# Perceiver layer on one core: context tiles turned by VectorE and a transfer through DRAM instead of by TensorE

## The reference, cut to what matters

```python
x = x + xattn(layernorm(x), ctx_1024, ...)     # 16 heads of 64, 16 batches
# inside xattn
ctx = layer_norm(context) * g + b              # [16, 1024, 256]
k, v = split(ctx @ Wkv)                        # 2 x 1024 columns
k = apply_rope(k, cos, sin)                    # [x1*cos - x2*sin, x2*cos + x1*sin]
attn = softmax(clip(q @ k.T / 8, -11, 11))     # per batch and head 64 x 1024
out = (attn @ v) @ Wo + bo
```

## Time and profile before

| | us |
|---|---|
| median of 3 runs (1255.79 to 1260.7) | 1257.02 |
| the profiled execution | 1255.76 |
| its span | 1254.0 |
| PE busy | 1226.5 (98% of the span) |
| DVE busy | 936.9 (75%) |
| ACT busy | 704.7 (56%) |
| POOL busy | 678.9 (54%) |
| granted TensorE clock, mean | 0.998 of full speed |

### The profile page before, as it was taken

How to read it: one execution, slowest core, us unless ns; L and a number is a source line. 1 busy time by engine, 2 the same in 40 slices (tenths; PEclk the granted TensorE clock), 3 DMA queues, 4 the chain that set the end, 5 groups by cost and what they waited for, 6 DMA issues and landing times.

```text
span 1254.0 us, 40596 instructions
## 1 busy us (share of the span) xinstructions
PE 1226.5 (98%) x16508; PEld 1027.6 (82%) x16508; DVE 936.9 (75%) x1924; ACT 704.7 (56%) x1359; POOL 678.9 (54%) x611
## 2 busy tenths in 40 slices
PE   7999999999999999999999999999999999999997
PEld 3678888888888888888888888888888788789997
DVE  6797877777887777877777787777777356768886
ACT  7756556555655655655655665665643233356664
POOL 3466666666576566566566566666554123333333
PEclk9999999999999999999999999999999999999999
DMA  6345444545445445445444444444545261566662
GB/s 235 66 99 114 99 107 110 107 100 114 101 98 114 104 108 115 103 98 113 105 106 105 108 101 105 111 106 102 132 99 130 88 219 36 187 178 194 205 186 73
DMA packets 96913, 149.95 MB, mean 120 GB/s; under 512 B 29452, under 2 KB 64728, under 8 KB 96600
## 3 DMA queue, kind: packets, MB, share of 16 engines
q1 hardware_dynamic: 92648, 143.14, 46.2%
q0 software_dynamic: 4080, 4.22, 1.7%
HBM read 66.20 MB, written 14.83 MB: 65 GB/s over the span
## 4 chain that ended last, share of the span: by engine, by line
PE 92%; ACT 2%; DVE 2%; DMA 2%; issue 1%; POOL 1%; SPq 0%; POOLq 0%; ACTq 0%; DVEq 0%
PE bank L1421 30%; PE bank L1451 28%; PE bank L1407 11%; PE bank L1759 6%; PE bank L1476 3%; PE bank L1431 2%; PE bank L1587 2%; PE bank L1809 2%; PE bank L1811 1%; PE bank L1810 1%; PE bank L1616 1%; PE bank L1659 1%; PE bank L1510 1%; DMA w_two<-in_L_ffn_W_dram 1%; PE bank L1640 1%
## 5 line engine op out<-in xcount | busy, mean ns | idle before, releaser
L568 POOL TENSOR_TENSOR kr<-kr,ksw 128x1024 f32<-128x1024 f32 x128 | 308.7, 2412 | 341.7 <-DVE pr L969 219.3
L1421 PE MATMUL bank<-ct,wk_hi 128*128 128x512 f32 x1024 | 331.7, 405 | 0.0
L1451 PE MATMUL bank<-p_hi,xc 128*128 128x512 f32 x1024 | 315.8, 390 | 0.0
L720 ACT ACTIVATE ctf<-bank,vecs 128x128 f32<-128x128 f32 x256 | 103.3, 453 | 333.5 <-PE bank L1431 333.5
L1451 PEld LDWEIGHTS bank<-p_hi,xc 128*128 128x128 f32 x1024 | 191.9, 188 | 39.9
L1421 PEld LDWEIGHTS bank<-ct,wk_hi 128*128 128x128 f32 x1024 | 182.3, 188 | 41.8
L1421 PE MATMUL bank<-ct,wk_lo 128*128 128x512 f32 x512 | 200.6, 392 | 0.0
L1451 PE MATMUL bank<-p_lo,xc 128*128 128x512 f32 x512 | 200.5, 392 | 0.0
L1001 DVE TENSOR_TENSOR kw<-bank,stab 128x512 f32<-128x512 f32 x256 | 175.7, 686 | 27.7 <-PE bank L1421 24.8
L992 DVE TENSOR_TENSOR p_lo<-pr,p_hi 128x1024 fp32r<-128x1024 f32 x128 | 184.3, 1440 | 1.8 <-ACT p_hi L707 1.8
L1009 DVE TENSOR_TENSOR ct<-ctf,ct 128x256 fp32r<-128x256 f32 x128 | 57.8, 452 | 170.6 <-ACT ct L725 170.6
(11 more groups left out here) (215 smaller groups left out, 1728.8 us busy)
## 6 DMA issues: line engine op xcount, KB each, us to landing
ksw<-kw SPq DMA_DIRECT2D x512, 128.0 KB
raw<-in_ctx_dram SPq DMA_DIRECT2D x64, 256.0 KB, 4.0
w_two<-in_L_ffn_W_dram SPq DMA_DIRECT2D x15, 1024.0 KB, 5.1
x_slots<-fill SPq DMA_DIRECT2D x128, 64.5 KB, 2.9
w_all<-in_L_ffn_W_dram SPq DMA_DIRECT2D x4, 2048.0 KB, 17.6
wo<-in_L_ffn_W_dram SPq DMA_DIRECT2D x7, 1024.0 KB, 5.2
lsum<-l_rows SPq DMA_DIRECT2D x64, 64.0 KB, 2.7
xs<-x_slots SPq DMA_DIRECT2D x23, 129.0 KB, 2.2
```

The costliest lines, as they stand in the source:

```text
L568: pool.tensor_tensor(kr[:, i], kr[:, i], ksw[:, i], ALU.add).then_inc(kr_done, 1)
L720: last = act.activation(ctf[:, k], psT[:, k * P:(k + 1) * P], ACT.Identity, bias=vecs[:, 3, k:k + 1], scale=vecs[:, 2, k:k + 1])
L1421: last = pe.matmul(psK[:, a * 512:(a + 1) * 512], l[:, k, w], ct[:, h % 3, r, k], start=(m == 0), stop=(m == len(parts) - 1))
L1451: last = pe.matmul(psZ[c], xc[:, slot_, l, t, cols], r[:, i, :, t], start=(f == 0 and m == 0), stop=(f == 1 and m == len(parts) - 1), skip ...
```

## The change

Tiles 0 to 7 (batch 1) are turned by TensorE as before. Tiles 8 to 127 take another way. VectorE turns the eight 32x32 blocks across and four down of the normalised tile, each within itself, into `xt` (`blocks_turned`, tile `j + 11`, between `weights_low` and `divided`). After every fourth tile, in steps with j % 4 = 1, SP writes `xt` to DRAM with four DMAs of 32 partitions in runs of 128 floats; these stand ahead of the key exchange of the step. Behind the exchange SP waits until they have landed and loads the half, now with the 256 values on the partitions, into `ctf` (2 x 512 floats per partition). In the next step (j % 4 = 2) ScalarE scales `ctf` in place and rounds it into `ct` high, and VectorE makes `ct` low of all 1024 floats at once. The columns of a half now stand in another order, which the cosine and sine multiplications undo by reading the keys in PSUM in runs of 32. Moments, shift and normalising run two steps earlier, context loads start two steps earlier, the loads of `wout_raw` and `bout_all` and the clearing of `vbd` move to the last steps.

```diff
+        x_turned = nc.dram_tensor("x_turned", [KC, P, HALF_S], F32, kind="Internal").ap()
+            xt = sb("xt", [P, D // HALF, HT, HALF], F32, turning)
+            ctf = sb("ctf", [P, KC, HALF_S], F32, turning)
...
@@ SP, step(j)
+                if due(j, 1) and (j + 7) // 4 < 2 * B:
+                    h = (j + 7) // 4
+                    sp.wait_ge(xt_done, HT * (h - 1))
+                    wait(sp, xt_moved, 80 * (h - 2))
+                    for i in range(4):
+                        sp.dma_start(x_turned[:, :, i * P:(i + 1) * P].rearrange("c (k p) s -> p (c k) s", p=HALF),
+                                     xt[i * HALF:(i + 1) * HALF].rearrange("p k t s -> p k (t s)")).then_inc(xt_moved, 16)
                 if there(j + 2):
                     ...
                         sp.dma_start(ksw[to:to + HALF, i], kw[of:of + HALF, i]).then_inc(sw_ld[i], 16)
+                if due(j, 1) and (j + 7) // 4 < 2 * B:
+                    h = (j + 7) // 4
+                    sp.wait_ge(xt_moved, 80 * (h - 2) + 64)
+                    wait(sp, ct_lo_done, HT * h)
+                    sp.dma_start(ctf[:], x_turned.rearrange("c p s -> p c s")).then_inc(xt_moved, 16)
...
@@ ScalarE, step(j)
-                if there(j + 9):
+                if 0 <= j + 9 < ST:
...
+                if due(j, 2) and (j + 6) // 4 < 2 * B:
+                    h = (j + 6) // 4
+                    act.wait_ge(xt_moved, 80 * (h - 1))
+                    for k in range(KC):
+                        last = act.activation(ctf[:, k], ctf[:, k], ACT.Identity, bias=vecs[:, 3, k:k + 1], scale=vecs[:, 2, k:k + 1])
+                    last.then_inc(ctf_done, 1)
+                    if h >= 3:
+                        act.wait_ge(k_ps, 2 * last_key(h - 3) + 2)
+                    act.wait_ge(ctf_done, ST + h - 1)
+                    act.copy(ct[:, h % 3, 0], ctf[:]).then_inc(ct_hi_done, HT)
...
@@ VectorE
+            def blocks_turned(j):
+                if ST <= j + 11 and there(j + 11):
+                    n = j + 11
+                    dve.wait_ge(xhat_done, n + 1)
+                    if n % HT == 0:
+                        wait(dve, xt_moved, 80 * (n // HT - 3) + 64)
+                    dve.transpose(xt[:, :, n % HT], raw[:, n // ST % 2, n % ST].rearrange("p (k s) -> p k s", s=HALF)).then_inc(xt_done, 1)
...
-                    dve.tensor_tensor(kw[:, i, cols], psK[:, cols], stab[:, places], ALU.mult).then_inc(kw_done, 1)
-                    dve.tensor_tensor(kr[:, i, cols], psK[:, cols], ctab[:, places], ALU.mult).then_inc(ku_done, 1)
+                    keys_ = psK[:, cols].rearrange("p (i t s) -> p t i s", t=HT, s=HALF)
+                    dve.tensor_tensor(by_tile(kw[:, i, cols]), keys_, by_tile(stab[:, places]), ALU.mult).then_inc(kw_done, 1)
+                    dve.tensor_tensor(by_tile(kr[:, i, cols]), keys_, by_tile(ctab[:, places]), ALU.mult).then_inc(ku_done, 1)
...
+                if due(j, 2) and (j + 6) // 4 < 2 * B:
+                    h = (j + 6) // 4
+                    dve.wait_ge(ct_hi_done, HT * (h + 1))
+                    dve.tensor_tensor(ct[:, h % 3, 1], ctf[:], ct[:, h % 3, 0].bitcast(F32), ALU.subtract).then_inc(ct_lo_done, HT)
...
@@ TensorE
             def turn_context(j):
-                if there(j):
+                if 0 <= j < ST:
...
-                    if due(j - 9, 7):
-                        pe.wait_ge(o_sum, (j - 16) // 4 * 2 + 1)
```

More of the change, by code:

```diff
@@ L83, in build @@
         fill = sb("fill", [P, D + 2])
+        with ExitStack() as turning:
+            xt = sb("xt", [P, D // HALF, HT, HALF], F32, turning)
+            ctf = sb("ctf", [P, KC, HALF_S], F32, turning)
         wout_raw = sb("wout_raw", [P, KC, D])
         bo_all = sb("bo_all", [P, D])
-        with ExitStack() as turning:
-            ctf = sb("ctf", [P, KC, P], F32, turning)
         bout_all = sb("bout_all", [P, D])
+        with ExitStack() as middle:
+            vbd = sb("vbd", [P, 2, AH, 2 * (AD + 1)], F32, middle)
+        h_lo_0 = sb("h_lo_0", [P, 2 * AH * 2 * (AD + 1)], F32R)
         vec_rows2 = sb("vec_rows2", [E * FT + 4, P])
@@ L91, in build @@
         feat_w = sb("feat_w", [P, 2, P])
-        with ExitStack() as middle:
-            vbd = sb("vbd", [P, 2, AH, 2 * (AD + 1)], F32, middle)
-        h_lo_0 = sb("h_lo_0", [P, 2 * AH * 2 * (AD + 1)], F32R)
         square = sb("square", [P, P])
@@ L390, in _ @@
             sp.dma_start(x_slots[E * TOK:, :], fill[:]).then_inc(fill_st, 16)
-            for r in range(KC):
-                for h in range(2):
-                    sp.dma_start(wout_raw[:, r, h * P:(h + 1) * P].rearrange("p (g d) -> p g d", d=AD),
-                                 Wout[r * P:(r + 1) * P, :].rearrange("p (g h d) -> p h g d", h=2, d=AD)[:, h]).then_inc(wout_ld, 16)
             sp.dma_start(vec_rows2[0:E * FT, :], b1.rearrange("e (f p) -> (e f) p", p=P)).then_inc(vec2_ld, 16)
@@ L422, in step @@
                     sp.dma_start(x_slots[j * N:(j + 1) * N, :], fill[o:o + N, :]).then_inc(fill_st, 16)
-                if j >= 0 and j % 2 == 0 and j // PAIRS + 2 < B:
-                    sp.wait_ge(xT_ps, j + 2)
-                    sp.wait_ge(x_lo_done, j + 2)
-                    context(j // PAIRS + 2, j % PAIRS // 2)
+                if j >= -2 and j % 2 == 0 and (j + 2) // PAIRS + 2 < B:
+                    if j + 2 < ST:
+                        sp.wait_ge(xT_ps, j + 4)
+                    else:
+                        sp.wait_ge(xt_done, j + 4 - ST)
+                    sp.wait_ge(x_lo_done, j + 4)
+                    context((j + 2) // PAIRS + 2, (j + 2) % PAIRS // 2)
             for j in range(-2, 0):
@@ L538, in _ @@
             pool.memset(cvec[:, 1:2], EPS)
-            pool.memset(vbd[:], 0.0).then_inc(vbd_ones, 1)
-            pool.wait_ge(vbd_ones, 1)
-            for b in range(2):
-                at = b * (AD + 1) + AD
-                pool.memset(vbd[b * N:(b + 1) * N, :, :, at:at + 1], 1.0).then_inc(vbd_ones, 1)
-                pool.wait_ge(vbd_ones, b + 2)
             for c in range(2):
@@ L681, in step @@
                     act.activation(pr_by_head, heads_by_tile, ACT.Exp, scale=SCALE).then_inc(exp_done, 1)
-                if there(j + 10) and j + 10 >= ST:
-                    i = (j + 10) % 2
-                    x_ = raw[:, (j + 10) // ST % 2, (j + 10) % ST]
-                    act.wait_ge(shift_done, j + 11 - ST)
-                    if j + 10 == ST:
+                if there(j + 12) and j + 12 >= ST:
+                    i = (j + 12) % 2
+                    x_ = raw[:, (j + 12) // ST % 2, (j + 12) % ST]
+                    act.wait_ge(shift_done, j + 13 - ST)
+                    if j + 12 == ST:
                         act.wait_ge(xhat_done, ST)
@@ L937, in normalised @@
             def normalised(j):
-                if 0 <= j + 10 < ST:
-                    n = j + 10
-                    dve.wait_ge(rstd_done, n + 1)
+                for n in range(max(j + 11, 0) if j > -10 else 0, min(j + 12, ST)):
+                    dve.wait_ge(rstd_done, (n // HT + 1) * ST)
                     dve.tensor_scalar(raw[:, 0, n], raw[:, 0, n], xl_mom[:, n, 0:1], xl_rsd[:, n:n + 1], ALU.subtract, ALU.mult).then_inc(xhat_done, 1)
             def shifts(j):
-                if ST <= j + 10 and there(j + 10):
-                    i = (j + 10) % 2
-                    dve.wait_ge(rstd_done, j + 11)
-                    if j + 10 >= ST + 2:
-                        dve.wait_ge(xhat_done, j + 9)
+                if ST <= j + 12 and there(j + 12):
+                    i = (j + 12) % 2
+                    dve.wait_ge(rstd_done, 2 * (j + 13))
+                    if j + 12 >= ST + 2:
+                        dve.wait_ge(xhat_done, j + 11)
                     dve.scalar_tensor_tensor(out=shift[:, i:i + 1], in0=mv[:, i, 0:1], scalar=-1.0, in1=rstd[:, i:i + 1],
@@ L952, in counted @@
             def counted(j):
-                if ST <= j + 11 and there(j + 11):
-                    n = j + 11
+                if ST <= j + 13 and there(j + 13):
+                    n = j + 13
                     b, t = n // ST, n % ST
@@ L1020, in step @@
                 weights_low(j)
+                blocks_turned(j)
                 divided(j)
```

88 lines of the change are left out of this document (50 added, 38 removed).

## The result

| | us |
|---|---|
| before, median of 16 runs (1255.34 to 1261.48) | 1257.95 |
| changed, median of 16 runs (1253.54 to 1274.22) | 1264.88 |
| ratio, with its 95% interval | 1.0045 [1.0024, 1.0065] |
| changed, the profiled execution | 1253.54, span 1251.8 |
| forecast (range) | 1243.0 (1228 to 1274) |

The changed kernel is 0.45% slower (0.2 to 0.7%), a difference too small to count, where 14 us (1.1%) of gain were forecast. One of the 16 runs (1274.22) is a slow one and is left out of the ratio. The profiled execution is the fastest of the 16, 11.3 us under their median, so I also read a second profile, taken with the first experiment (1262.71 us, span 1261.0).

A forecast was written before the change was run, and what follows sets the result against it. The prediction took PE, busy 98% of the span, as the bound. Turn removal -27.6 us plus new stall 13.5 gave -14.1: from 1255.76 to 1241.7, with the median 1.3 above, 1243.0 us; range 1228 to 1274.

The forecast's parts named there:

- PE's turn: Last in each PE step; removing it was to save 0.23 us for 120 of 128 tiles, 27.6 us.
- Block turn: On VectorE, after p_lo: taken as 0.42 us a tile, hidden up to about 0.9 us.
- Issue of a write: Block writes on SP ahead of the exchange: 0.59 us each; with 0.78, stall 30 us in all.
- The 200 us a quad to which I gave 1 in 100: Block writes to DRAM as slow as a strided transposing DMA: kernel about 6000 us longer, chance 1 in 100.
- The writes' landing: Four block writes, j % 4 = 1: landed 2.9 or 3.9 us after the last issue, before the next block turn.
- VectorE's wait: Before the next half's first block turn, for landed writes: nothing of its own, or about 0.2 us a quad.
- the ends: Earlier moments, moved small loads and vbd clearing beside other work: 0 us, bounds -1 to +2.
- stalls in other steps: PE idle at steps other than before the scores of j % 4 = 3: none forecast.
- the stall before T3: PE waiting for kr before the scores of j % 4 = 3: 0.45 us a quad, 13.5 us over 30 quads.
- The landing of the exchange: Key exchange, j % 4 = 1: landed at most 4.86 us after issue, in late cases for instance 5.82.
- The rival "given back": Slow write issue or exchange packets held up 0.7 us cancel the gain: 1251 to 1263 us, chance 0.18.
- The rival "slower": SP's queue in j % 4 = 1 makes the exchange the bound: 1275 us, +18 us, chance 0.22.

The follow-up runs named there:

- the first experiment: The changed kernel as it is, measured again for a second trace: median 1260.14 us, ratio 1.0028.
- No turn at all: The kernel before with TensorE's turn left out for tiles 8 to 127 and nothing in its place: 1232.17 us, ratio 0.9798.
- the best version: Changed kernel, two block writes on SP before clearing and context load, two on ScalarE, small loads divided between steps 118 and 119: 1235.46 us, ratio 0.9828.

## Why the prediction was wrong

Right first. **PE's turn**: 0.23 us in plain steps held exactly (6.98 to 6.76). In the step with outputs it is 0.40 (8.09 to 7.69), which the earlier trace rows could not show as a turn's price: a quad gains 1.09 us instead of 0.92. **Block turn**: 0.435 us against 0.42. **Issue of a write**: 0.46 us in the median (2.0 for four) against 0.61, so the unknown that I called the one that counts was no problem. The 200 us a quad to which I gave 1 in 100 did not come either. **The writes' landing**: the turn at T1 + 9.1, the upper of my two values (8.0 to 9.0); but VectorE's wait is 1.9 us on the mean and up to 3.7, not under 1.5. **Idle place**: before T3's scores, released by POOL, as listed.

What failed, and by how much in the spans of the two profiles: the ends 7.1 and 9.1 us, stalls in other steps 4.8 and 6.6, the stall before T3 2.5 and 8.0; the turn gave 2.3 more than forecast. Together that is the 11.9 and 21.1 us by which the forecast of -14.1 missed, within 0.3. By steps:

*The landing of the exchange, kept at its value before the change.* This is the term of the sum that was mis-sized. The prediction took 4.86 us for 73% of the quads and 5.82 for the rest, on the mean 5.1. The 4.86 of the earlier trace rows is only a bound, the smallest of the 21 quads in which VectorE released GpSimd, and it hit by luck: the landings read from the semaphore have a mean of 4.83 us in the kernel before, 5.0 to the start of the sum. In the changed kernel they have 5.37 and 5.40 (4.2 to 7.2). The forecast let the exchange land as before although four new transfers are in flight with it; that they would hold it up stood only in the rivals. Put into my own sum with its two starts, 5.77 and 6.7, the landings of the kernel before give 10.9 us of stall in 28 quads, those of the changed one 21.5 and 22.8. Measured: 16.0 and 21.5. So the 13.5 of the forecast came close in the first profile because it took the exchange's starts later than they were.

*Stalls in other steps, put at nothing.* 4.8 and 6.6 us. I took VectorE's delay as ending with its quad. It doesn't: when `kr` is late on GpSimd, it overlaps `p_lo` (2.55 us at 606.18 instead of 1.33), the block turn and the context's low part come later, and with them the next `kw` and its exchange, which starts at T2 + 5.9 in the median instead of T2 + 4.87. In the second profile 3.0 of the 6.6 us are two steps at a granted clock of 0.81.

*VectorE's wait "costs nothing of its own".* Nearly so: by the table above the clipping adds 1.4 and 2.6 us to what the exchange makes. But it would make 8.6 and 11.6 alone, so with the exchange early again it is the next to stall, and the remedy had to make both early.

*Ends, 0 with bounds -1 to +2.* Too low: 2.0 to 2.2 us up to step 7; 2.0 to 2.5 in steps 120 to 126, most of it the small loads ahead of an exchange, which I had put "beside other work" without looking at the queue; 2.9 to 4.6 behind them, about what the low clock can cost there. No turn at all has 2.0 of the last too, so not all of it is the change's.

*The clock.* No term at all. It is no further loss beside these but a part of them: up to 3.3 and 5.4 us of the ends, and 3.0 of the stalls in the second profile. The prediction also took 1.3 us from the profiled execution to the median; the first profile lay 11.3 under it.

The sum from parts measured: -29.9 (turn) + 20.8 (stalls) + 2.2 + 2.0 + 2.9 = -2.0 us in the first profile, against -2.2 in its span; -29.9 + 28.1 + 2.0 + 2.5 + 4.6 = +7.3 in the second, against +7.0. The rival "given back" came nearest (1264.88 and 1260.14, for 1251 to 1263). The slow issue that it named was no cause. An exchange held up by 0.7 us was one, with 0.5 to 0.6 us, by whichever transfer. The rival "slower" had the right place and overrated the price.

Open: why the first scores come 1.5 us later (53.04 against 51.53), why the stretch behind the cross attention has more of the low clock in every version, and which transfer holds the exchange up. No run was made for any of them.

## What to carry to other kernels

When a change uses up spare time, don't take the duration of the transfer it now waits for from one case. Where another engine was the releaser, the case gives only an upper bound, and where the transfer was, only the late ones are seen: 5.35 to 6.51 us to the start of the sum, median 5.80, in 9 of 30 quads here, against 5.0 on the mean of all. Then ask what the change adds beside that transfer, and price a longer landing in the forecast itself. When two inputs of one operation are both late, undoing one shows little, and moving a transfer's start does not show that its landing moved: read both inputs' times. Before a queue gets new work ahead of an urgent transfer, look at what stands before both and isn't urgent: moving two issues was worth about 20 us here (1260.14 to 1240.57, ratios 1.0028 and 0.9868).

## What the runs showed of the hardware

VectorE's `p_lo`, whose two inputs lie in SBUF, stretched from 1.33 to 2.55 us while GpSimd's `kr` (605.25 to 607.65) was running, and ended 1.1 us behind it; its products from PSUM (`kw`, `kr`, 0.68 us each) did not stretch beside GpSimd's sum. The Trainium skill, "SBUF — State Buffer", section "Who interferes with whom", says that a VectorE instruction with two SBUF inputs contends with a GpSimd instruction that reads SBUF, and that the order of issue decides who blocks. This trace agrees: GpSimd's sum had begun first, and `p_lo` took 1.2 us more. The mean of `p_lo` rose from 1440 ns before to 1590 ns, and is 1499 in the best version.

ScalarE's scaling of 128x512 floats took 0.76 us each with the input in SBUF (1.52 for two at 620.60), where the copy of 128x512 from PSUM takes 0.58; I had used the latter. The two differ in the operation too (one scales and adds a bias from memory), so no run parts what the source costs.

The exchange of 4 x 32 partitions, started at T1 + 4.87 each time, landed 4.78 us after its issue in the median of 28 quads before, 5.83 and 6.16 with block writes issued by ScalarE shortly ahead of it, and 4.49 where two writes stood on each queue and the clearing and a context load came behind the exchange. The mean busy share of the DMA engines in the cross attention rose from 0.48 to 0.59 with the change.
